# Late modulation blocks of a conditioned transformer block gathered in one step of the first body, and part of the first q stack issued from ScalarE

## The chip, the cores and the metric

One core of a Trainium2 chip. The metric is device microseconds of one execution, from the first to the last instruction with what lies around them; the median of several executions is compared.

## The reference, cut to what matters

x is 16 batches of 224 tokens by 512; the context 16 x 750 x 512; all is fp32. Per batch:

```python
c_proj = silu(c) @ W_mod + b_mod          # (16, 512) @ (512, 3072): 6 blocks of 512
shift_a, scale_a, gate_a, shift_m, scale_m, gate_m = split(c_proj, 6)
x_norm = ln(x) * (1 + scale_a) + shift_a
q, k, v = split(x_norm @ W_qkv + b_qkv, 3)             # 16 heads of 32
x = x + gate_a * (softmax(q k^T * scale) v @ W_proj + b_proj)
x = x + cross_attention(ln(x), ln(context))
h = gelu((ln(x) * (1 + scale_m) + shift_m) @ W_mlp1 + b_mlp1)
return x + gate_m * (h @ W_mlp2 + b_mlp2)
```

shift_a and scale_a are needed before anything else. gate_a is needed at the first residual of the self-attention; gate_m, shift_m and scale_m only much later. These four are the *late* blocks here.

## The kernel before, in words

The program has a self-attention phase (the first 700 us or so), a cross-attention phase and an MLP phase, with hand-written seams. Only the self-attention phase is touched. There each of five engines (SP for DMA issues, PE, DVE, ACT, POOL) has its own program, in order, and they meet at semaphores; nothing is planned by a tool. The order is written out as a *start* (16 steps h that make k, q and v of batch 0) and then *bodies*, one per batch, of 16 steps h each, one step per head. In step h of body b PE does, in this order: the transposed scores of an earlier head (`score_t`, six heads behind), a product for another batch from the table FILL (k, q and v of batch b+1, the projection of b-1, the cross q of b-2), the scores of head h+1 (`score`), every fourth step the attention output and row sums of four heads (`pv`, `sums`), at h = 12 and 13 the transposes of x of batch b+2 (`turn_x`), every fourth step the turn of the row maxima. Bodies 0 and 1 have no products of the cross q, body 0 has no projection, so their last steps (10 to 15, and 13 to 15) are thin.

Scores need k and q *stacked*: three pieces of 32 rows per head group, copied by DMA out of `natq` and `nat` into `qst` and `kst` (`stack`, L431). The first heads of batch 0 wait for one semaphore each (`first_q[j]`).

What x of the next batches goes through: `turn_x` on PE, `modulate` on DVE, `high_x` on ACT (L1141), `low_x` on POOL (L1287). At the end of a body POOL also has `sum_p` (L1295) for each head, and from body 1 on the residual of the batch before, four operations (L1303, L1305). The product k of the next batch, the first of the next body, waits for `low_x`.

The modulation: `modulation_rows(i)` (L732) multiplies silu of the conditioning, 128 x 16 four times, by a 512 x 512 block of W_mod, and gives 16 rows of 512 in a PSUM bank. Blocks 0 and 1 are made in the start. Block 2 (gate_a) is made at the end of the start, just before the first score; block 3 (gate_m) in the last step of body 0; blocks 4 and 5 (shift_m, scale_m) in steps 13 and 14 of body 1. `gate_rows` (L1009) adds the bias on DVE; `mlp_row` copies; `turn_rows` (L739) turns the last two on PE, and their bias rows at the start; `keep_bias`, `keep_modulation` store them. SP loads block 2 early, block 3 in body 0 after the first maxima, blocks 4 and 5 at the end of body 0, and stores the two gates as soon as each is there (`store_gates`). The k product of batch 2, third step of body 1, waits for the second gate rows (`rows_done` 2).

## Time and profile before

| what | value |
|---|---|
| median of 3 runs | 2616.03 us (2615.39 to 2621.15) |
| the profiled execution | 2619.34 us, span 2617.5 us |
| PE busy / DVE / ACT / POOL | 2578.0 / 1694.1 / 1126.6 / 1275.6 us |
| mean granted clock of TensorE | 0.991 |
| start of body 0, 1, 2 (first score of the batch on PE) | 43.63, 74.93, 125.71 us |

How to read it: times are microseconds from the start of the span. PE is TensorE's matmul side, PEld its weight loads. A bracket at the end of a timeline row is the time that the engine stood idle before it and what released it. An f32 matmul shows as two records; records on PE overlap in the pipeline, so a block's length is read from its start to the start of the next. The granted clock is a share of 2.4 GHz: 1.00 or 0.50.

### The profile page before, as it was taken

What the parts mean: (1) busy time and instruction counts of PE and PEld (TensorE: products, weight loads), DVE (VectorE), ACT (ScalarE), POOL (GpSimd) and SP (SyncE); (2) the same over time, 40 slices, a digit from 0 to 9 for tenths busy, and PEclk for the clock granted to TensorE, in tenths of its full rate; (3) what the DMA queues carried; (4) which work ended last, traced back from release to release, by engine and by line L of the source; (5) the groups of instructions that cost most, each with busy time, mean ns of one, the idle gap of its engine ahead of it and who ended that gap; (6) DMA issues with size and microseconds to landing.
All of it is one profiled execution on the core that took longest, in us unless ns stands there. A gap on an engine that the chain in (4) does not pass through costs nothing.

```text
span 2617.5 us, 50236 instructions
## 1 busy us (share of the span) xinstructions
PE 2578.0 (98%) x18696; PEld 2133.6 (82%) x18696; DVE 1694.1 (65%) x3399; ACT 1126.6 (43%) x2192; POOL 1275.6 (49%) x1426
## 2 busy tenths in 40 slices
PE   8999999999999999999999999999899999999999
PEld 6688888888788888888888888887678888888887
DVE  6677777777757777777777777776764444444442
ACT  4354454444535555555555555554552221212111
POOL 1445455454436777777777777775421121220230
PEclk9999999999899999999999999999899999999999
DMA  8454545555454444444444444434521111111110
GB/s 225 128 136 125 135 120 130 129 129 132 137 148 111 115 115 112 113 114 112 117 114 116 119 113 115 121 90 102 153 94 45 37 44 34 45 49 37 45 53 17
DMA packets 193045, 269.89 MB, mean 103 GB/s; under 512 B 34788, under 2 KB 112612, under 8 KB 192788
## 3 DMA queue, kind: packets, MB, share of 16 engines
q1 hardware_dynamic: 187116, 254.16, 36.9%
q0 software_dynamic: 3264, 7.92, 0.9%
q10 hardware_dynamic: 2424, 4.61, 0.7%
q8 instruction: 150, 2.46, 0.4%
q14 instruction: 91, 0.75, 0.1%
HBM read 111.11 MB, written 36.77 MB: 56 GB/s over the span
## 4 chain that ended last, share of the span: by engine, by line
PE 69%; DVE 1%; issue 0%; DMA 0%; ACT 0%; SPq 0%; DVEq 0%; ACTq 0%
PE late_tr_ps L1793 7%; PE late_sc_ps L1779 7%; PE late_or_ps L1806 5%; PE late_even_ps L72 5%; PE late_sc_ps L72 5%; PE late_even_ps L73 5%; PE late_even_ps L74 5%; PE late_sc_ps L74 5%; PE late_sc_ps L73 5%; PE late_odd_ps L72 3%; PE late_odd_ps L74 3%; PE late_odd_ps L73 3%; PE late_tr_ps L74 2%; PE late_tr_ps L72 2%; PE late_tr_ps L73 2%; PE late_odd_ps L1740 1%
## 5 line engine op out<-in xcount | busy, mean ns | idle before, releaser
L2138 ACT ACTIVATE cross_prT<-late_tr_ps 125x448 f32<-125x448 f32 x759 | 403.0, 544 | 273.5 <-PE late_tr_ps L1793 264.6
L1965 DVE TENSOR_REDUCE cross_parts<-late_sc_ps 112x1 f32<-112x500 f32 x512 | 335.5, 663 | 221.8 <-PE late_sc_ps L1779 220.7
L2211 POOL TENSOR_TENSOR cross_part<-cross_prT 125x448 f32<-125x448 f32 x232 | 271.2, 1169 | 214.6 <-ACT cross_prT L2138 176.9
L1295 POOL TENSOR_TENSOR self_psum<-self_prT 112x224 f32<-112x224 f32 x256 | 179.0, 699 | 328.3 <-ACT self_prT L1160 319.5
L1793 PE MATMUL late_tr_ps<-cross_qst,cross_kst 98*125 98x224 f32 x1536 | 309.5, 284 | 5.4 <-ACT cross_prT L2138 4.4
L1793 PEld LDWEIGHTS late_tr_ps<-cross_qst,cross_kst 98*125 98x125 f32 x1536 | 255.3, 188 | 55.8 <-ACT cross_prT L2138 16.5
L2613 ACT ACTIVATE mlp_hv<-late_sc_ps,mlp_b 128x512 f32<-128x512 f32 x112 | 77.0, 687 | 511.5 <-PE late_sc_ps L74 497.1
L2213 POOL TENSOR_TENSOR cross_part<-cross_part,cross_prT 125x448 f32<-125x448 f32 x232 | 268.5, 1157 | 18.2
L1779 PE MATMUL late_sc_ps<-cross_kst,cross_qst 96*112 96x500 f32 (+1 forms) x1024 | 262.2, 337 | 5.2 <-PEq L99 3.3
L2527 DVE CAST mlp_hT_h<-mlp_hv 128x512 fp32r<-128x512 f32 x112 | 55.9, 499 | 301.8 <-ACT mlp_hv L2613 301.8
L1160 ACT ACTIVATE self_prT<-self_st_ps 112x448 f32<-112x448 f32 x256 | 138.4, 541 | 167.6 <-PE self_st_ps L628 166.4
L1779 PEld LDWEIGHTS late_sc_ps<-cross_kst,cross_qst 96*112 96x112 f32 x1024 | 165.2, 179 | 20.1 <-issue 3.5
L908 DVE TENSOR_REDUCE self_nmax<-self_sc_ps 112x2 f32<-112x448 f32 x256 | 154.5, 614 | 33.3 <-PE self_sc_ps L599 33.2
L72 PE MATMUL late_sc_ps<-mlp_xT_l,mlp_w_h 128*128 128x512 f32 x448 | 175.8, 393 | 0.0
L74 PE MATMUL late_sc_ps<-mlp_xT_h,mlp_w_h 128*128 128x512 f32 x448 | 175.2, 391 | 0.0
L73 PE MATMUL late_sc_ps<-mlp_xT_h,mlp_w_l 128*128 128x512 f32 x448 | 175.0, 391 | 0.0
L1967 DVE TENSOR_REDUCE cross_parts<-late_sc_ps 112x2 f32<-112x500 f32 x256 | 170.2, 665 | 0.0
L2215 POOL TENSOR_TENSOR cross_psum<-cross_part 125x224 f32<-125x224 f32 x232 | 155.6, 671 | 18.2
L1806 PE MATMUL late_or_ps<-cross_prT,cross_vt 125*32 125x224 f32 x2784 | 143.7, 354 | 0.0
L72 PE MATMUL self_pj_ps<-self_xT_l,self_wqkv_h 128*128 128x224 f32 x512 | 140.6, 275 | 2.4 <-DVE self_wm_gates L1009 1.4
L74 PE MATMUL self_pj_ps<-self_xT_h,self_wqkv_h 128*128 128x224 f32 x512 | 140.6, 275 | 0.0
L73 PE MATMUL self_pj_ps<-self_xT_h,self_wqkv_l 128*128 128x224 f32 x512 | 140.3, 274 | 0.0
(343 smaller groups left out, 6870.9 us busy)
## 6 DMA issues: line engine op xcount, KB each, us to landing
cross_kst<-cross_nat_h SPq DMA_DIRECT2D x508, 93.8 KB, 2.2
cross_kst<-cross_nat_l SPq DMA_DIRECT2D x254, 93.8 KB, 2.2
cross_qst<-qc SPq DMA_DIRECT2D x192, 112.0 KB, 2.5
cross_c_in<-in_context SPq DMA_DIRECT2D x78, 224.0 KB
self_kst<-self_nat_h SPq DMA_DIRECT2D x128, 112.0 KB, 2.3
self_qst<-self_natq_h SPq DMA_DIRECT2D x128, 112.0 KB, 3.0
self_x_in<-in_x SPq DMA_DIRECT2D x16, 448.0 KB, 3.8
self_kst<-self_nat_l SPq DMA_DIRECT2D x64, 112.0 KB, 2.2
```

What stands on the lines that cost most here:

```text
L72: pe.matmul(out, lhs[0], rhs[1], start=first, stop=False)
L73: pe.matmul(out, lhs[1], rhs[0], start=False, stop=False)
L74: return pe.matmul(out, lhs[0], rhs[0], start=False, stop=last)
L1295: pool.tensor_tensor(psum[:, j], prT[:, j, 0], prT[:, j, 1], ALU.add).then_inc(p_summed, 1)
L1779: last = pe.matmul(sc_ps[u][0:QN, at:at + cn], qst[g][0:TERMS * HD, j, t * QN:(t + 1) * QN], kst[g][j][0:TERMS * HD, c0:c0 + cn], start=Tr ...
L1793: last = pe.matmul(bank(h, c)[0:SN, m * N:(m + 1) * N], kst[g][j][:, kt * SN:(kt + 1) * SN], qst[g][:, j, :], start=True, stop=True)
L1806: last = pe.matmul(or_ps[HD * j:HD * j + HD, 0:N], vt[b.par][:, kt, h * HD:h * HD + HD], prT[:, slot(h), kt], start=kt == 0, stop=kt == ST ...
L1965: dve.tensor_reduce(parts[:, g % 2, j, u, 0:1], sc_ps[u][0:QN, 0:SHALF[0]], AX_X, ALU.max, negate=True).then_inc(maxed, 1)
L1967: dve.tensor_reduce(parts[:, g % 2, j, :, 1], sc_ps[u][0:QN, 0:QT * SHALF[1]].rearrange("p (t k) -> p t k", t=QT), AX_X, ALU.max, negate=T ...
L2138: act.activation(probabilities(b, h)[:, 2 * c:2 * c + 2], bank(h, c)[0:SN, 0:2 * N].rearrange("p (k t) -> p k t", k=2), ACT.Exp).then_inc( ...
L2211: pool.tensor_tensor(part[:], prT[:, j, 0:2], prT[:, j, 2:4], ALU.add).then_inc(pre_summed, 1)
L2213: pool.tensor_tensor(part[:], part[:], prT[:, j, 4:6], ALU.add).then_inc(pre_summed, 1)
```

## The change

Blocks 2 to 5 are now made together, at the beginning of step 10 of body 0, in one PSUM bank: silu is padded with zeros from 16 to 32 columns, and block j goes to partitions 32j to 32j+31. One DVE addition over 128 x 512 adds all biases (DMA'd into a zeroed tile before), PE turns the whole in four 128 x 128 transposes in step 15 of body 0, and DVE keeps shift and scale there. The separate blocks at the end of the start, in body 0 step 15 and in body 1 steps 13 and 14, the bias turn in the start and the stores in between are gone. Blocks 3, 4 and 5 are loaded through ACT's DMA queue in steps 2, 5 and 10 of the start. Of the first batch's q stack SP issues heads 0 and 1 of each group; heads 2 and 3 are issued by ACT in steps 8 and 9 of the start. ACT's `high_o` in body 1 waits for the gates to be stored and the rows to be turned.

```diff
-        MOD_BANK = (sc_ps[0], sc_ps[1], or_ps, pj_ps[1], pj_ps[0], pj_ps[1])
+        MOD_BANK = (sc_ps[0], sc_ps[1])
+        LATE = range(2, 6)
@@ sync
             def store_gates():
+                sp.wait_ge(rows_done, 1)
                 for n in range(2):
-                    sp.wait_ge(rows_done, n + 1)
-                    sp.dma_start(gates[n], wm_gates[0:B, n, 0]).then_inc(gates_out, 16)
+                    sp.dma_start(gates[n], late_rows[HD * n:HD * n + B]).then_inc(gates_out, 16)
+
+            def load_late_bias():
+                sp.wait_ge(padded, 2)
+                for j, i in enumerate(LATE):
+                    m = MOD[i]
+                    sp.dma_start(late_bias[HD * j:HD * j + B], b_mod[m * H:(m + 1) * H].rearrange("(a n) -> a n", a=1).broadcast_to([B, H])).then_inc(late_bias_in, 16)
...
-                if b.c == 0:
-                    load_mod(3)
...
                 if b.c == 0:
-                    load_mod(4)
-                    load_mod(5)
                     store_gates()
...
-            stack(Batch(0), q_l, natq, qst, q_stacked, (0, 0, 1))
+            stack(Batch(0), q_l, natq, qst, q_stacked, (0, 0, 1), range(2))
@@ tensor
...
-                    pe.wait_ge(bm_kept, 1)
...
+                if kind == "k" and c == 0 and part == 0 and o.c == 2:
+                    pe.wait_ge(rows_done, 1)
                 if kind == "k" and c == 1 and part == 0 and o.c == 2:
-                    pe.wait_ge(rows_done, 2)
-                if kind == "k" and c == 1 and part == 0 and o.c == 3:
                     pe.wait_ge(mod_done, 2)
...
+            def late_modulation_rows():
+
+                pe.wait_ge(v_done, v_count(Batch(1), 0))
+                for k in range(KC):
+                    for j, i in enumerate(LATE):
+                        if k == 0:
+                            pe.wait_ge(wm_in[j], 16)
+                        last = pe.matmul(pj_ps[0][HD * j:HD * j + HD, :], silu[:, k], mod_raw[i][:, k], start=k == 0, stop=k == KC - 1)
+                last.then_inc(mod_ps, 1)
...
+            def turn_late_rows():
+                pe.wait_ge(rows_done, 1)
+                pe.wait_ge(v_done, v_count(Batch(1), 1))
+                for k in range(KC):
+                    last = pe.transpose(pj_ps[1][:, k * P:(k + 1) * P], late_rows[:, k * P:(k + 1) * P], ident[:])
+                last.then_inc(mod_turned, 1)
...
                 for h in range(NH):
+                    if b.c == 0 and h == 10:
+                        late_modulation_rows()
                     for o, l in late(b, h, att, prv):
                         score_t(o, l)
+                    if b.c == 0 and h == NH - 1:
+                        turn_late_rows()
...
-                    if b.c == 1 and h in (13, 14):
-                        pe.wait_ge(proj_done, h - 12)
-                        modulation_rows(h - 9)
...
-                    if b.c == 0 and h == NH - 1:
-                        pe.wait_ge(v_done, Batch(1).n(2, 2))
-                        modulation_rows(3)
-                    if b.c == 1 and h == 15:
-                        pe.wait_ge(mlp_rows, 2)
-                        turn_rows(pj_ps[1], lambda n, k: wm_mlp[0:B, n, 0, k * P:(k + 1) * P], mod_turned)
...
-            modulation_rows(2)
             score(Batch(0), 0)
@@ vector
...
+                    if b.c == 0 and h == 10:
+                        keep_late_rows()
+                    if b.c == 0 and h == NH - 1:
                         keep_modulation()
...
+            def keep_late_rows():
+                dve.wait_ge(mod_ps, 3)
+                dve.wait_ge(late_bias_in, 16 * len(LATE))
+                dve.tensor_tensor(late_rows[:], pj_ps[0][:], late_bias[:], ALU.add).then_inc(rows_done, 1)
@@ scalar
+            def stack_first_q(j):
+                act.wait_ge(q_l, Batch(0).n(2, 2))
+                for r, s in enumerate((0, 0, 1)):
+                    act.dma_start(qst[HD * r:HD * r + HD, 0, :, j].bitcast(F32), natq[s][HD * j:HD * j + HD].bitcast(F32)).then_inc(first_q[j], 16)
...
             def high_o(b, g):
                 if g == 0:
                     wait(act, proj_ps, b.n(2, 0))
+                if g == 1 and b.c == 0:
+                    act.wait_ge(gates_out, 32)
+                    act.wait_ge(mod_turned, 2)
...
                     evict(*f)
+                if h in (2, 5, 10):
+                    load_mod({2: 3, 5: 4, 10: 5}[h])
+                if h in (8, 9):
+                    stack_first_q(h - 6)
@@ gpsimd
+            pool.memset(silu[:], 0.0).then_inc(padded, 1)
+            pool.memset(late_bias[:], 0.0).then_inc(padded, 1)
```

## Rows read from the trace of the kernel before

**Rows 1.** The page, section 1: TensorE busy, share of the span.
```profile
PE 2578.0 (98%) x18696; PEld 2133.6 (82%) x18696; DVE 1694.1 (65%) x3399; ACT 1126.6 (43%) x2192; POOL 1275.6 (49%) x1426
```

**Rows 2.** Timeline of PE: start, duration (us), line, operation, out<-in, records.
```profile
40.09 3.61 PE L732 MATMUL self_or_ps<-self_wm_gates,self_silu 128*16 128x512 f32 x8
...
75.55 6.21 PE L732 MATMUL self_pj_ps<-self_wm_gates,self_silu 128*16 128x512 f32 x8
...
116.20 3.61 PE L732 MATMUL self_pj_ps<-self_wm_mlp,self_silu 128*16 128x512 f32 x8
...
126.08 0.66 PE L739 MATMUL self_pj_ps<-shared_ident,self_wm_mlp 16*128 16x16 f32 x8
```

**Rows 3.** The same timeline: attention output and its sums, four heads at once.
```profile
65.15 0.96 PE L645 MATMUL self_or_ps<-self_prT,self_vt 112*32 112x224 f32 x16
65.93 0.56 PE L652 MATMUL self_or_ps<-self_psum,self_ones 112*32 112x224 f32 x8
```

**Rows 4.** Timeline of SP, its DMA issues before the first body.
```profile
37.85 0.59 SPq L431 DMA_DIRECT2D self_kst<-self_nat_h  x1
...
39.84 0.61 SPq L431 DMA_DIRECT2D self_qst<-self_natq_l  x1
...
41.84 0.61 SPq L431 DMA_DIRECT2D self_qst<-self_natq_l  x1
```

**Rows 5.** Timeline of PE: the scores of heads 0, 1 and 3 of batch 0.
```profile
43.63 0.47 PE L599 MATMUL self_sc_ps<-self_kst,self_qst 96*112 96x224 f32 x2
...
45.27 0.37 PE L599 MATMUL self_sc_ps<-self_kst,self_qst 96*112 96x224 f32 x2
...
48.82 0.46 PE L599 MATMUL self_sc_ps<-self_kst,self_qst 96*112 96x224 f32 x2 [0.29 <-DMA self_qst<-self_natq_l]
```

**Rows 6.** Timelines of ACT, then POOL: what x of batch 1 goes through.
```profile
40.20 0.58 ACT L1153 COPY self_vt<-self_pj_ps 112x512 f32<-112x512 f32 x1 [2.59 <-PE self_pj_ps L74]
40.68 1.03 ACT L1141 CAST self_xT_h<-self_xv 128x448 fp32r<-128x448 f32 x2
...
41.39 2.34 POOL L1287 TENSOR_TENSOR self_xT_l<-self_xv,self_xT_h 128x448 fp32r<-128x448 f32 x2 [11.49 <-ACT self_xT_h L1141]
```

**Rows 7.** DMA issues from 36 to 40 us, then from 52 to 56 us; last column us to landing.
```profile
self_kst<-self_nat_h SPq DMA_DIRECT2D x3, 112.0 KB, 2.2
self_qst<-self_natq_l SPq DMA_DIRECT2D x1, 112.0 KB, 2.7
...
self_kst<-self_nat_h SPq DMA_DIRECT2D x3, 112.0 KB, 5.4
```

**Rows 8.** Timeline of PE at the end of body 0.
```profile
69.53 0.60 PE L562 MATMUL self_tx_ps<-shared_ident,self_x_in 112*128 112x112 f32 x4 [0.88 <-DVE self_xv L839]
...
71.58 1.72 PE L645 MATMUL self_or_ps<-self_prT,self_vt 112*32 112x224 f32 x16 [0.41 <-DVE self_ou L925]
...
83.33 0.37 PE L599 MATMUL self_sc_ps<-self_kst,self_qst 96*112 96x224 f32 x2
```

**Rows 9.** Timeline of POOL, end of body 0.
```profile
73.20 2.69 POOL L1287 TENSOR_TENSOR self_xT_l<-self_xv,self_xT_h 128x448 fp32r<-128x448 f32 x2
```

**Rows 10.** Busy time by stretch: PE, PEld, DVE, ACT, POOL, granted clock (share), DMA.
```profile
70.00:72.00 2.00, 1.43 (x14) 0.91 (x16) 1.90 (x4) 0.61 (x3) 0.00 (x0) 0.65 0.57 128
...
80.00:82.00 2.00, 2.00 (x6) 0.46 (x5) 0.00 (x0) 0.00 (x0) 0.00 (x0) 0.79 1.05 408
```

**Rows 11.** Timeline of PE in body 1, step 2.
```profile
87.05 0.35 PE L72 MATMUL self_pj_ps<-self_xT_l,self_wqkv_h 128*128 128x224 f32 x1 [1.39 <-DVE self_wm_gates L1009]
```

**Rows 12.** Timeline of POOL, end of body 1: first and last of eight operations, none waiting between.
```profile
115.27 1.28 POOL L1303 TENSOR_TENSOR self_y<-self_y,self_gate 112x512 f32<-112x512 f32 x1
...
122.81 2.38 POOL L1287 TENSOR_TENSOR self_xT_l<-self_xv,self_xT_h 128x448 fp32r<-128x448 f32 x2
```

**Rows 13.** Timeline of PE around it: turn of x, and the score behind the first k product.
```profile
115.31 0.55 PE L562 MATMUL self_tx_ps<-shared_ident,self_x_in 112*128 112x112 f32 x4
...
128.31 0.37 PE L599 MATMUL self_sc_ps<-self_kst,self_qst 96*112 96x224 f32 x2
```

More of the change, by code:

```diff
@@ L180, in self_phase @@
         x_in = sb("x_in", [QN, QT, H])
-        cond, cond_e, cond_d, cond_i, silu = (sb(name, [P, KC, B]) for name in ("cond", "cond_e", "cond_d", "cond_i", "silu"))
+        cond, cond_e, cond_d, cond_i = (sb(name, [P, KC, B]) for name in ("cond", "cond_e", "cond_d", "cond_i"))
         ROWS = TERMS * HD + 2
@@ L197, in self_phase @@
         wm_gates = nc.alloc_sbuf_tensor_at("self_wm_gates", [P, 2, KC, H], F32, offset=late_at)
-        bm_gates = [nc.alloc_sbuf_tensor_at(f"self_bm_gates{n}", [B, H], F32, offset=oT_at + 4 * N * (1, KC + 1)[n]) for n in range(2)]
+        late_bias, late_rows = (nc.alloc_sbuf_tensor_at(f"self_late_{name}", [P, H], F32, offset=oT_at + 4 * N * at)
+                                for name, at in (("bias", 1), ("rows", KC + 1)))
         wm_mlp = nc.alloc_sbuf_tensor_at("self_wm_mlp", [P, 2, KC, H], F32, offset=wqc_at)
-        bm_t = sb("bm_t", [P, 2 * KC, B])
+        silu = sb("silu", [P, KC, HD])
         nat = [sb(f"nat_{s}", [P, KC, N], F32R) for s in "hl"]
@@ L273, in self_phase @@
         mod_ps, mod_rows, mod_turned, mod_done, rows_done, gates_out = (sem(s) for s in ("mod_ps", "mod_rows", "mod_turned", "mod_done", "rows_done", "gates_out"))
-        bm_gates_in, bm_turned, bm_kept, mlp_rows, even_ones, odd_ones = (sem(s) for s in ("bm_gates_in", "bm_turned", "bm_kept", "mlp_rows", "even_ones", "odd_ones"))
+        late_bias_in, padded, even_ones, odd_ones = (sem(s) for s in ("late_bias_in", "padded", "even_ones", "odd_ones"))
         filled, shaped = sem("filled"), sem("shaped")
@@ L545, in _ @@
             load_x(Batch(1))
-            for n, m in enumerate((GATE_A, GATE_M)):
-                sp.dma_start(bm_gates[n][:], b_mod[m * H:(m + 1) * H].rearrange("(a n) -> a n", a=1).broadcast_to([B, H])).then_inc(bm_gates_in, 16)
+            load_late_bias()
             load_w("p", w_proj, 0)
@@ L727, in modulation_rows, with turn_first_rows @@
                 for k in range(KC):
-                    if i < 2 and k % 2 == 0:
+                    if k % 2 == 0:
                         pe.wait_ge(first_in[i][k // 2], 16)
-                    elif k == 0:
-                        pe.wait_ge(wm_in[i - 2], 16)
-                    last = pe.matmul(MOD_BANK[i][0:B, :], silu[:, k], mod_raw[i][:, k], start=k == 0, stop=k == KC - 1)
+                    last = pe.matmul(MOD_BANK[i][0:B, :], silu[:, k, 0:B], mod_raw[i][:, k], start=k == 0, stop=k == KC - 1)
                 last.then_inc(mod_ps, 1)
-            def turn_rows(bank, src, done):
+            def late_modulation_rows():
[6 more added lines that the diff above has]
+                last.then_inc(mod_ps, 1)
+            def turn_first_rows():
                 for n in range(2):
@@ L738, in turn_rows @@
                         at = (n * KC + k) * B
[L739 to L740 removed]
+                        last = pe.transpose(st_ps[0][:, at:at + B], vt[0:B, 0, n, k * P:(k + 1) * P], ident[0:B, 0:B])
+                last.then_inc(mod_turned, 1)
[4 more added lines that the diff above has]
+                    last = pe.transpose(pj_ps[1][:, k * P:(k + 1) * P], late_rows[:, k * P:(k + 1) * P], ident[:])
+                last.then_inc(mod_turned, 1)
             def body(b, att, nxt, prv, old):
                 for h in range(NH):
+                    if b.c == 0 and h == 10:
+                        late_modulation_rows()
                     for o, l in late(b, h, att, prv):
                         score_t(o, l)
+                    if b.c == 0 and h == NH - 1:
+                        turn_late_rows()
                     work = fills(b, h, "kqvpc")
@@ L974, in body @@
                         low_w(3 * KC + h - 2)
-                    if b.c == 1 and h == 0:
-                        gate_rows(3)
-                    if b.c == 1 and h in (13, 14):
-                        mlp_row(h - 9)
-                    if b.c == 1 and h == 15:
+                    if b.c == 0 and h == 10:
+                        keep_late_rows()
+                    if b.c == 0 and h == NH - 1:
                         keep_modulation()
@@ L1018, in keep_first_modulation @@
                 dve.wait_ge(mod_done, 1)
-            def columns(bank):
-                return bank[:, 0:2 * KC * B].rearrange("p (m b) -> p m b", b=B)
-            def keep_bias():
-                dve.wait_ge(bm_turned, 1)
-                dve.tensor_copy(bm_t[:, 0:KC], columns(st_ps[1])[:, 0:KC])
-                dve.tensor_scalar(bm_t[:, KC:2 * KC], columns(st_ps[1])[:, KC:2 * KC], 1.0, None, ALU.add).then_inc(bm_kept, 1)
             def keep_modulation():
                 dve.wait_ge(mod_turned, 2)
-                dve.wait_ge(bm_kept, 1)
-                dve.tensor_tensor(mod_t[:, 2 * KC:4 * KC], columns(pj_ps[1]), bm_t[:], ALU.add).then_inc(mod_done, 1)
+                shift, scale = (pj_ps[1][:].rearrange("p (k r) -> p k r", k=KC)[:, :, HD * j:HD * j + B] for j in (2, 3))
+                dve.tensor_copy(mod_t[:, 2 * KC:3 * KC], shift)
+                dve.tensor_scalar(mod_t[:, 3 * KC:4 * KC], scale, 1.0, None, ALU.add).then_inc(mod_done, 1)
             a = Batch(0)
```

25 lines of the change are left out of this document (7 added, 18 removed).

## The prediction

> **What bounds the kernel.** I read the page first: TensorE is busy 98% of the span [rows 1], so only what PE does or waits for counts, and in the first 130 us each removed instruction has to be asked whether PE gets through earlier or merely meets its next wait. Then the timeline of PE over the blocks that go [rows 2], the rows that price their replacement [rows 3], and around each place the queue that feeds PE there: SP's issues [rows 4, 7], ACT and POOL in the start [rows 6], POOL at the end of bodies 0 and 1 [rows 9, 12]. Last the windows, for the clock [rows 10].
>
> The sum is made against the profiled execution, 2619.34 us, which is 3.3 us above the median of 2616.03. A difference of 0.2%, 5.2 us, is about what a measurement of this kernel can tell from none.
>
> **The modulation work on PE.** A block of four f32 matmuls takes 3.54 us at full clock: from 40.09 to the score at 43.63 [rows 2, 5]. Four go. That of body 0 took 6.14 us, 75.55 to 81.69, because PE had the half clock of 1.2 GHz there [rows 2, 10]. The turn in body 1, about 0.6 us, goes as well [rows 2]. Added is one block of 16 matmuls, four at a time on four strips of columns. No row shows it at 512 columns; its bounds are 3.5 us, if four strips run together, and 4 x 3.54 = 14.2 us, if they don't. The nearest row is the attention output: eight f32 matmuls of 224 columns, in the same order over four strips, start at 65.15 and the sums follow at 65.93 [rows 3]. That is 0.78 us; one by one they would take 8 x (3.54 / 4) x 224/512 = 3.1 us. So four run as one, and I take 3.6 us. The four transposes I put at 0.5 us (four transposes of a smaller tile show 0.55 us [rows 13]).
>
> The Trainium skill (TensorE: Matmul & The Clock Gate, "Measured speedup vs the span model") gives three column strips a speedup of 2.38, not 3; carried to four, my estimate from it is 3.2, the block 4.5 us and the sum 0.9 us more. The trace speaks against it: 3.1 / 0.78 is a factor of 4.
>
> If each removed piece were worth its length, PE would gain 3.54 + 6.14 + 2 x 3.54 + 0.6 = 17.4 us, plus the wait below, minus 4.1. It isn't; three places show why.
>
> **Place 1, the first score.** Without block 2 PE would reach score 0 at 40.1 instead of 43.63. But the last k piece is issued at 37.85 and lands 2.2 us later, at 40.1; the last piece of q head 0 is issued at 39.84 and lands 2.7 us later, at 42.5 [rows 4, 7]. So at best 1.1 us is left. Next comes k of batch 1, which needs `low_x` of batch 1. Before, ACT evicts v at 40.20, does both `high_x` from 40.68, and POOL ends at 41.39 + 2.34 = 43.7, just as PE arrives [rows 6]. Now ACT's queue holds, between that evict and `high_x`, three stack issues and one load. An issue of a stack costs SP 0.6 us [rows 4]; on ACT no row of this stage shows it, so bounds are nothing and 0.6; I take 0.6, the same DMA. Then `high_x` starts at about 42.6, its second half's `low_x` ends at 45.5, and the k product, whose last half (0.67 us) waits for it, ends at 46.2 instead of at 45.27 [rows 5]: 0.9 us **later**. The wait of 0.29 us at head 3 goes [rows 5]. Net +0.6 us. Bounds: -1.4 us (ACT's issues cost nothing, so only q head 0 counts), and +4 us: block 4's load of 1 MB is now under way while the first stacks move. Where block 3's load went just ahead of k stacks, from 52.88, they landed 5.4 us after issue instead of 2.2 [rows 7]; 3.2 us more on q head 0 puts score 0 at 45.7, and q head 1, issued at 41.84, at 47.7.
>
> The Trainium skill (DMA: Bandwidth & Descriptors, "Issuing engines are not separate DMA queues") says that DMAs from SP and ACT run on the same 16 DMA engines and interleave, so that a second issuer saves issue time alone. By it the q rows of heads 2 and 3 delay those of heads 0 and 1, and the sum goes towards +2. The landings of [rows 7] show transfers of one queue that delay each other; no row shows two queues.
>
> **Place 2, end of body 0.** The late block comes in at 64.55 or so and moves all behind it by 3.6 us. Behind it PE waits for chains that don't shorten: 0.88 us for DVE, 0.41 us for the attention output [rows 8]. In the last step block 3 has covered POOL: `low_x` of batch 2 ends at 73.20 + 2.69 = 75.9 [rows 9], and PE came to k of batch 2 only behind it. Without the block, k's second half waits for 75.9 + 3.6 = 79.5 and the step ends at 80.2, not at 83.33 [rows 8]: -3.1 us, and of the 6.14 us removed that is all after the late block is paid. This holds at full clock. Had PE had it before too, the step would have ended at 83.33 - 4.6 = 78.7 (block 3 2.6 us shorter, and some 2.0 us of what stands between 71.58 and 75.55), so against an execution without the slow stretch this place **costs** 1.5 us.
>
> **The wait in body 1.** PE stood 1.39 us for the gate rows, which came behind a reciprocal on DVE [rows 11]. Those rows are now made in body 0: -1.4 us. New is ACT's wait for the stored gates before `high_o` of group 1. SP stores them after the last maxima, about 80; even a landing of 4 us ends near 84, ACT is due there at about 82.7 (behind the second k product), and its next exponentials are asked for two steps of 1.6 us on: nothing on PE. DVE's addition over 128 x 512 (0.68 us as the 16-row one) lies beside attention output and sums. Padding, bias rows and the removed bias turn lie under the first loads and DVE's weight splits: nothing.
>
> **Place 3, end of body 1.** Blocks 4 and 5 and the turn fill 7.7 us there. Yet POOL runs from 115.27 to 122.81 + 2.38 = 125.2 without a gap: two residuals, two sums, both `low_x` [rows 12]; it starts with PE's transposes at 115.31 and doesn't hang on the blocks. PE would be ready for k of batch 3 at about 121.8: 126.08 [rows 2] less the two blocks, 119.0, and some 2.8 us of waits for DVE that the blocks hid (in body 0 0.88, 0.41 and more [rows 8]). It waits, k's second half starts at 125.2, the step ends at 125.9 instead of 128.31 [rows 13]: -2.4 us of 7.7.
>
> **Sum at full clock:** 2619.34 + 0.6 - 3.1 - 1.4 - 2.4 = 2613.0 us (rounded).
>
> **The clock.** Before, the granted clock fell to half once here, near 70.6, after waits of 0.88 us and less in the thin end of body 0, and stayed so to near 80.8: the windows give 0.65 for 70 to 72 and 0.79 for 80 to 82 [rows 10]. With less work and longer waits both thin ends get sparser: in body 1 PE would idle some 5 us of 9. I take it that the clock falls there. Inside the thin end POOL's wait hides that; the k products behind it run at half speed until it is given back. From both ends: nothing, and half of 10.2 us (a stretch as long as the one before, all of it on products), 5.1. I take the middle, 2.6. In body 0 the same may return and outlast 80.2; there at most half the stretch does, so the bounds are 0 and 2.6, and I take 0.8, since POOL's wait hides its beginning. Forecast: 2613.0 + 3.4 = **2616.4 us**.
>
> **Rivals.** (1) *Removed work counts in full*: PE-bound throughout, POOL and stacks catch up. It gives 2619.34 - 17.4 - 1.4 + 4.1 = 2604.6. For it speaks PE's 98%; against it [rows 9, 12], which no shorter PE moves. 0.2, with half-way outcomes below 2610.8. (2) *Slower: the strips don't run together* at 512 columns. Place: step 10 of body 0; price up to 14.2 - 3.6 = 10.6, so 2626.6; it decides from a block of 8.8 us on. [rows 3] speaks against it. 0.05. (3) *The change doesn't give the q rows earlier*: the load through ACT delays the first stacks, place 1 at +4, and 2619.8; with both slow stretches at their long ends 2624. 0.25 in all, 0.1 of it beyond 2621.3. The forecast has 0.5.
>
> **Numbers.** Low end: full clock throughout and place 1 at -1.4 give 2611.0, and a part of rival 1 reaches to 2608. High end: place 1 at +4 and half the long stretches, 2622. Faster by over 0.2% (below 2610.8) 0.21, within 0.64, slower 0.15.
>
> **What would show it.** Right: the late block takes 3.5 to 3.7 us; score 0 starts after 42.5, and PE or `low_x` of batch 1 is later than before; k of batches 2 and 3 stands behind POOL's `low_x` by about 1.5 us and 2 to 3; the 1.39 us wait is gone; granted clock 0.5 near the end of body 1. Wrong: PE goes into k of batch 3 without an idle bracket, or the first score of body 2 comes more than 10 us earlier than before, or the late block takes over 5 us.

## The result: 7.5 us slower, all of it lost before score 4 of batch 0

| | before | after |
|---|---|---|
| median of 14 runs each, us | 2615.52 (2612.52 to 2621.15) | 2623.02 (2621.85 to 2624.91) |
| ratio after / before | | 1.0028, 95% interval 1.0021 to 1.0035 |
| profiled execution, us | 2619.34 | 2624.22 |
| its span, us, and granted clock | 2617.5, 0.991 | 2622.3, 0.989 |

Predicted were 2616.4 us and a range of 2608 to 2622, with 0.64 for "no difference". The kernel is slower by 0.28%, which is the outcome "slower by over 0.2%" that had 0.15, and outside the range. The interval is 0.07% to either side, so this comparison tells smaller differences than the 0.2% that the prediction took for its limit.

The page's section 1 of after, for [rows 1]:

```profile
PE 2570.8 (98%) x18684; PEld 2137.7 (82%) x18684; DVE 1691.4 (65%) x3395; ACT 1126.6 (43%) x2192; POOL 1277.4 (49%) x1428
```

PE is busy for 7.2 us less and the span is 4.8 us longer: 12 us of idle time are new in this execution. The timeline of PE in after tells where (columns as in [rows 5], which holds these scores of before):

```profile
48.51 0.68 PE L603 MATMUL self_sc_ps<-self_kst,self_qst 96*112 96x224 f32 x2 [7.86 <-DMA self_qst<-self_natq_l]
...
52.39 0.72 PE L603 MATMUL self_sc_ps<-self_kst,self_qst 96*112 96x224 f32 x2 [0.64 <-DMA self_qst<-self_natq_l]
...
58.00 0.37 PE L603 MATMUL self_sc_ps<-self_kst,self_qst 96*112 96x224 f32 x2
...
73.67 0.62 PE L742 MATMUL self_pj_ps<-self_wm_gates,self_silu 128*32 128x512 f32 x2
...
77.24 0.46 PE L631 MATMUL self_st_ps<-self_qst,self_kst 98*112 98x224 f32 x2
...
84.28 1.23 PE L647 MATMUL self_or_ps<-self_prT,self_vt 112*32 112x224 f32 x16 [0.75 <-DVE self_ou L934]
...
86.70 1.05 PE L756 MATMUL self_pj_ps<-shared_ident,self_late_rows 128*128 128x128 f32 x4
...
89.83 0.37 PE L603 MATMUL self_sc_ps<-self_kst,self_qst 96*112 96x224 f32 x2
...
120.20 0.55 PE L566 MATMUL self_tx_ps<-shared_ident,self_x_in 112*128 112x112 f32 x4
...
128.35 0.34 PE L72 MATMUL self_pj_ps<-self_xT_l,self_wqkv_h 128*128 128x224 f32 x1 [1.44 <-POOL self_xT_l L1296]
...
130.90 0.57 PE L603 MATMUL self_sc_ps<-self_kst,self_qst 96*112 96x224 f32 x2
...
136.82 0.37 PE L603 MATMUL self_sc_ps<-self_kst,self_qst 96*112 96x224 f32 x2
```

Score 0 comes 4.9 us later than in [rows 5], behind a wait of 7.86 us for q rows; score 1 comes 7.1 us later, score 3 9.2 us. Score 4 starts at 59.57 against 50.49, 9.1 us later. From there the lag shrinks: 6.5 us at 89.83 (83.33 in [rows 8]), 4.9 at 120.20 and 2.6 at 130.90 ([rows 13] for both). Then it grows once more, to 5.0 at 136.82 (131.83 before), about the difference of the spans.

Of the 9.1 us, 0.5 were there before any of this: the transposes of x in step 8 of the start began at 38.72 in after and at 38.21 in before. Over all profiled executions that point lies between 38.21 and 40.03, also for kernels with the same instructions up to there (38.21 in before, 39.02 in g2), so times of score 4 are compared below from that point on. By that the start costs 8.6 us.

Busy time by stretch in after (columns as in [rows 10]):

```profile
44.00:48.00 4.00, 0.00 (x0) 0.00 (x0) 0.00 (x0) 0.53 (x2) 2.25 (x2) 0.50 1.12 230
48.00:52.00 4.00, 3.24 (x14) 3.00 (x14) 0.62 (x1) 0.00 (x0) 0.00 (x0) 0.50 1.07 310
...
128.00:132.00 4.00, 3.42 (x18) 3.27 (x19) 1.48 (x6) 0.12 (x1) 3.56 (x6) 0.65 0.63 193
132.00:136.00 4.00, 4.00 (x21) 4.00 (x21) 2.73 (x6) 1.92 (x5) 0.66 (x1) 0.50 0.63 186
```

PE does nothing at all from 44 to 48 while the DMA engines are full (the last column but one). The half level of 1.2 GHz stands from about 44, some 3 us into the wait, to about 57.4; before had 2.4 GHz there throughout.

Why the rows are late shows in the DMA views of after. First the queues in 32 to 36 us (packets, MB, share of 16 engines), where q1 is SP's and q10 is ACT's, with one line of the issues of this stretch:

```profile
q10 hardware_dynamic: 670, 1.34, 99.0%
q1 hardware_dynamic: 6, 0.02, 1.3%
...
self_kst<-self_nat_h SPq DMA_DIRECT2D x5, 112.0 KB, 5.6
```

Then issues of 40 to 44 us (median us to landing in the last column):

```profile
self_wm_mlp<-in_w_mod ACTq DMA_DIRECT2D x1, 1024.0 KB, 11.3
...
self_qst<-self_natq_l SPq DMA_DIRECT2D x2, 112.0 KB, 7.5
```

SP issued a k stack every 0.6 us in the first of these, and in 4 us only six packets of its queue moved. The loads of 1 MB on ACT's queue had the engines almost to themselves. The k stacks land 5.6 us after issue and the last pieces of the q stacks 7.5, against 2.2 and 2.7 in [rows 7].

ACT's and POOL's timelines in after, for [rows 6]:

```profile
40.70 1.31 ACTq L1111 DMA_DIRECT2D self_qst<-self_natq_h  x2
42.05 0.68 ACTq L1111 DMA_DIRECT2D self_qst<-self_natq_l  x1
42.77 0.64 ACTq L1115 DMA_DIRECT2D self_wm_mlp<-in_w_mod  x1
43.50 1.03 ACT L1143 CAST self_xT_h<-self_xv 128x448 fp32r<-128x448 f32 x2 [2.23 <-issue]
...
44.21 2.33 POOL L1296 TENSOR_TENSOR self_xT_l<-self_xv,self_xT_h 128x448 fp32r<-128x448 f32 x2 [13.77 <-ACT self_xT_h L1143]
```

### The profile page after: what moved, and what is told of

Same layout as the page of the kernel before. It is cut to its first block, busy times and chain, and to the rows that moved or that the text cites. A ratio compares the mean times of both kernels' runs of the same rounds, so it can differ in the third digit from the quotient of the medians.

```text
span 2622.3 us, 50208 instructions
## 1 busy us (share of the span) xinstructions
PE 2570.8 (98%) x18684; PEld 2137.7 (82%) x18684; DVE 1691.4 (65%) x3395; ACT 1126.6 (43%) x2192; POOL 1277.4 (49%) x1428
## 4 chain that ended last, share of the span: by engine, by line
PE 68%; SPq 1%; DVE 1%; issue 0%; DMA 0%; ACT 0%; DVEq 0%
PE late_tr_ps L1804 7%; PE late_sc_ps L1790 6%; PE late_or_ps L1817 5%; PE late_sc_ps L72 5%; PE late_even_ps L72 5%; PE late_sc_ps L74 5%; PE late_sc_ps L73 5%; PE late_even_ps L74 5%; PE late_even_ps L73 5%; PE late_odd_ps L72 3%; PE late_odd_ps L74 3%; PE late_odd_ps L73 3%; PE late_tr_ps L74 2%; PE late_tr_ps L72 2%; PE late_tr_ps L73 2%; PE late_odd_ps L1751 1%
```

## The experiments

Each of the fourteen kernels has the median of 11 executions (f1 of 6, f2 of 9); before is given with the median of the same session. "Score 4" is the start of the fifth score of batch 0 in the one profiled execution, "from the transposes" the same counted from the transposes of x in step 8 of the start.

### The queues, one at a time

**e1: loads of blocks 3 to 5 back on SP.** After, with

```
# ACT, start
-                if h in (2, 5, 10):
-                    load_mod({2: 3, 5: 4, 10: 5}[h])
# SP, body 0, behind place_maxima(b, 0)
+                    for i in (3, 4, 5):
+                        load_mod(i)
```

> The changed kernel with one thing different: the loads of blocks 3, 4 and 5 go back to SP's queue, behind the first row maxima of body 0, where block 3's load stood before. Theory L (the 1 MB loads in ACT's queue in the start run ahead of SP's stacks, which then land 5 to 8 us after issue): the stacks land 2.2 to 3 us after issue again, score 0 starts between 42.5 and 43.7 us instead of 48.5, PE has no half clock near 50, and the time is 2613 to 2616, that is 7 to 10 us under the changed kernel and 0 to 2 us under the kernel before. Theory Q (it is the q rows of heads 2 and 3 in ACT's queue that delay those of heads 0 and 1): score 0 stays behind 46 us and the time at 2619 or more.

**e2: q rows back on SP,** the loads stay on ACT's queue:

```
-                if h in (8, 9):
-                    stack_first_q(h - 6)
-            stack(Batch(0), q_l, natq, qst, q_stacked, (0, 0, 1), range(2))
+            stack(Batch(0), q_l, natq, qst, q_stacked, (0, 0, 1))
```

> The changed kernel with the first batch's q stack all on SP again, the loads of blocks 3 to 5 still in ACT's queue. Theory L: q head 0 still lands 6 us or more after issue, score 0 starts at 46 to 49, the half clock follows, the time stays at 2621 to 2625. Theory Q: score 0 comes to about 43 us, the time to 2614 to 2617.

**e3 and e4: each transfer put alone into the kernel before.** e3 adds `stack_first_q` for heads 2 and 3 on ACT and cuts SP's stack to two heads; e4 adds ACT's three loads in steps 2, 5 and 10 of the start and drops SP's.

> The kernel before with only the q rows of heads 2 and 3 issued by ACT; modulation and loads as before. Theory L: score 0 starts within 0.5 us of 43.6, the wait of 0.29 us at head 3 goes, low_x of batch 1 ends some 2 us later than 43.7 and costs PE about 1 us; time within 1.5 us of the kernel before. Theory Q: score 0 at 45 or later, time 2 us or more above the kernel before.

> The kernel before with only the loads of blocks 3, 4 and 5 moved to ACT's queue in steps 2, 5 and 10 of the start; all modulation work where it was, the q stack on SP. Theory L: the stacks land 5 us or more after issue, score 0 starts at 46 to 49 us although block 2 stands before it, PE waits 3 to 5 us for it; time 4 to 9 us above the kernel before. Theory Q: nothing changes, within 1 us of the kernel before.

**f5: both transfers back on SP,** block 2 still out of the start (e1's and e2's edits together).

> The kernel after, with both transfers put back on SP's queue: all q rows of batch 0 as in the kernel before, and the loads of blocks 3 to 5 behind the first maxima of body 0. Block 2 stays out of the start. If the 9.1 us lost by score 4 come from what ACT's queue carries (both the loads and the q rows): q head 0 lands near 42.5, score 0 starts there behind a wait of about 2 us, score 4 starts at 49.5 to 50.5 instead of 59.57 (e1, with the q rows alone still on ACT's queue, had 54.62), and the median is near 2615.3, about 4.4 below e1's. Rival (the removed block itself is the loss: the wait that it covered brings half the granted clock whatever the queues do): half clock in the windows from 42 to 52, score 4 at 52.5 or later, median at 2618 or above.

| | loads | q rows of heads 2, 3 | block 2 in the start | median, us | before in that session | ratio, interval | score 4, us | from the transposes, us |
|---|---|---|---|---|---|---|---|---|
| after | ACT | ACT | no | 2623.02 | 2615.52 | 1.0028, 1.0021 to 1.0035 | 59.57 | 20.85 |
| e2 | ACT | SP | no | 2619.72 | 2615.71 | 1.0014, 1.0006 to 1.0023 | 56.13 | 17.76 |
| e1 | SP | ACT | no | 2619.72 | 2615.71 | 1.0013, 1.0004 to 1.0022 | 54.62 | 15.36 |
| f5 | SP | SP | no | 2616.45 | 2616.56 | 1.0003, 0.9994 to 1.0012 | 52.13 | 12.64 |
| e4 | ACT | SP | yes | 2621.99 | 2615.71 | 1.0023, 1.0014 to 1.0032 | 57.71 | 18.70 |
| e3 | SP | ACT | yes | 2620.73 | 2615.71 | 1.0017, 1.0008 to 1.0026 | 52.48 | 13.68 |
| before | SP | SP | yes | | | 1 | 50.49 | 12.28 |

With both transfers on SP no loss is left that the medians can show, and 0.4 of the 8.6 us in the trace. Putting one of the two back on SP gives 3.3 us of median (e1, e2 against after). The one that then remains is 3.3 us of median above f5 as well, but by the ratios that is 0.10 to 0.11%, with intervals that overlap. The traces part them: from the transposes to score 4 the loads cost 5.1 us (e2 against f5), the q rows 2.7 (e1 against f5), and the two sum to 7.8 of the 8.2 between f5 and after. My expectation for one cause was wrong: I had set the loads against the q rows, and both hold. For f5, 1.3 us of its score 4 at 52.13 instead of 49.5 to 50.5 is the later start; the half clock that its rival named is there, the rival's 2618 or more is not.

e3 and e4 have each transfer with the rest of the change absent, and both are slower than before: by 5.0 and 6.3 us of median, by 1.4 and 6.4 in the trace up to score 4. For e3 the two don't agree. Its profiled execution was its fastest (2616.87 us; the other ten go from 2618.35 to 2622.81), so where the rest of its 5.0 us goes is not shown. That the two medians sum to 11.3 and not to 7.5 stays open with it.

The waits at the first scores, from the timelines of PE of e1, e2, e4 (score 1) and f5:

```profile
45.42 0.69 PE L606 MATMUL self_sc_ps<-self_kst,self_qst 96*112 96x224 f32 x2 [4.21 <-DMA self_qst<-self_natq_l]
```
```profile
46.76 0.69 PE L603 MATMUL self_sc_ps<-self_kst,self_qst 96*112 96x224 f32 x2 [6.45 <-DMA self_qst<-self_natq_l]
```
```profile
50.44 0.71 PE L595 MATMUL self_sc_ps<-self_kst,self_qst 96*112 96x224 f32 x2 [3.04 <-DMA self_qst<-self_natq_l]
```
```profile
43.56 0.43 PE L606 MATMUL self_sc_ps<-self_kst,self_qst 96*112 96x224 f32 x2 [2.12 <-DMA self_qst<-self_natq_l]
```

How the q rows alone do it shows in the queues and issues of 40 to 44 us of e3, and below them the one queue of before in the same stretch:

```profile
q10 hardware_dynamic: 530, 0.43, 48.9%
q1 hardware_dynamic: 495, 0.46, 47.9%
...
self_qst<-self_natq_h SPq DMA_DIRECT2D x4, 112.0 KB, 4.1
self_qst<-self_natq_h ACTq DMA_DIRECT2D x2, 112.0 KB, 4.0
```
```profile
q1 hardware_dynamic: 874, 0.70, 80.4%
```

Here two queues with the same stacks share the engines evenly: the rows of heads 2 and 3, which are needed last, move beside those of heads 0 and 1, and all land after about 4 us where one queue took 2.3. More moves in the 4 us (0.90 MB against 0.71), but not what is needed first: the second queue takes the order away.

There is a second part. SP's first two issues of q stacks, in e3 and then in e4:

```profile
39.29 2.00 SPq L431 DMA_DIRECT2D self_qst<-self_natq_h  x2
```
```profile
39.29 1.32 SPq L431 DMA_DIRECT2D self_qst<-self_natq_h  x2
```

Where ACT issues its q stacks in the same stretch they take SP 1.78 to 2.12 us (after, e1, e3, f1, f2); in the other kernels, e2 and e4 with full DMA engines among them, 1.32. So the third piece of q head 0 is also issued some 0.7 us later.

### What the exposed wait costs by itself

**f4: f5 with work in block 2's place,** 16 f32 matmuls of 128 columns that nobody reads, before score 0:

```
+            filler(pe, or_ps, ident, 16)
             score(Batch(0), 0)
```

> f5 with 16 plain f32 matmuls of 128 columns (32 passes, about 3.6 us by the 0.114 us a pass of f1) before the first score, in the place of block 2. If the removed block is worth what it hid: score 0 at 43.7, score 4 at 50.5 as in the kernel before, median within 1 us of f5's. Rival (the exposed wait starts the half clock): f5 is slower than this one by 2 us or more.

Measured: 2616.56 us (ratio 0.9999, 0.9990 to 1.0008), f5's 2616.45. Score 0 started at 44.49, score 4 at 51.67, and from the transposes score 4 took 12.45 us for f5's 12.64. f5's profile does have a stretch at half clock behind its wait of 2.12 us (0.68 in 44 to 48, 0.90 in 48 to 52). Counted from the transposes its score 0 is 1.2 us earlier than f4's (4.07 against 5.27), and from score 0 to score 4 it is 1.4 us slower (8.57 against 7.18): the half clock takes back what the earlier score gave. Block 2 was worth nothing in the start, neither as work to remove nor as cover, as long as the stacks came on time.

**f1: after, with 36 such matmuls in the wait of 7.86 us.**

> The kernel after, with 36 plain f32 matmuls of 128 columns on TensorE between the last product of the start and the first score: they write a bank that nobody reads and lie inside the wait of 7.86 us. Theory C (the exposed wait makes the granted clock fall, and that carries about half of the 9.1 us lost by score 4): score 0 still starts near 48.5, the windows from 44 to 60 us show a granted clock near 1.0, score 4 starts near 56 instead of 59.57, and the median is near 2619.5 (3.5 below after's 2623.0). Rival D (scores 1 to 4 wait for their stacks, so the clock hides behind DMA): score 4 stays within 1 us of 59.5, more idle brackets for DMA appear before scores 1 to 3, and the median stays at 2622 to 2623.

```profile
54.05 0.46 PE L609 MATMUL self_sc_ps<-self_kst,self_qst 96*112 96x224 f32 x2 [2.48 <-DMA self_qst<-self_natq_l]
```
```profile
52.00:56.00 4.00, 1.95 (x13) 1.95 (x14) 0.62 (x1) 0.00 (x0) 0.00 (x0) 0.88 0.46 115
56.00:60.00 4.00, 4.00 (x28) 4.00 (x27) 2.09 (x5) 1.31 (x3) 0.00 (x0) 0.70 0.00 0
```

Measured: 2624.73 us over six executions (ratio 1.0031, 1.0019 to 1.0044), no gain. The clock stayed full over the whole wait (windows 40 to 52 at 1.00), and then PE stood 2.48 us for head 1's rows: at half clock the product between scores 0 and 1 had only filled that wait. Score 4 started at 60.43, but this start was 1.3 us later as a whole (the transposes ahead at 40.03 instead of 38.72), so 0.4 us were gained. So theory C falls: the clock is not half of the 9.1 us. Up to score 1 the landing of head 1's rows sets the time (7.1 us), whatever the clock is. Only the 2.0 us from there to score 4 (7.18 us in after from score 1 to 4, 5.22 before) are the clock's, and f1, with 6.38, lost 1.2 of them again in a new half-clock stretch behind its new wait.

### The parts that the prediction had priced

**g2: the gate row's addition moved out of body 1,** in the kernel before:

```
-                    if b.c == 1 and h == 0:
+                    if b.c == 0 and h == NH - 1:
                         gate_rows(3)
```

> The kernel before, with the second gate row's addition on DVE done at the end of body 0 instead of in step 0 of body 1. If the 1.39 us wait of body 1 is lost time by itself (my term for it): the wait is gone, and the median is 1.4 below before's, near 2614.3. Rival: the wait turns up at the next place, and the median stays within 0.4 of before's 2615.7.

Measured: 2614.16 us, 1.3 below before's 2615.50 in that session; ratio 0.9997, 0.9989 to 1.0006. Its timeline shows no idle bracket between 80 and 112 us, where [rows 11] has 1.39. The size is as expected, but the interval takes in no change, so it isn't shown by the times.

**g4: g2, with blocks 4 and 5 together on two strips** in step 13 of body 1, start and loads as before:

```
+                for k in range(KC):
+                    for i in (4, 5):
...
+                        at = HD * (i - 4)
+                        last = pe.matmul(pj_ps[0][at:at + B, :], silu[:, k], mod_raw[i][:, k], start=k == 0, stop=k == KC - 1)
```

> The kernel before, with the gate row as in g2, and blocks 4 and 5 taken together on two strips of columns in step 13 of body 1 (one block of 3.54 us instead of two); start, loads and q rows as in before. If place 3 is as I priced it (POOL's low_x sets the end of body 1, at most 2.4 us to be had) and the clock holds: TensorE stands some 0.5 to 1.2 us for low_x before the second half of k of batch 3, score 4 of body 2 starts 3.8 us before the kernel before's 135.06, at 131.3, and the median is near 2611.9. Rival 1: the whole 3.54 us counts, 2610.8 and no wait for POOL. Rival 2: the thinner end costs the clock its full level, a stretch at half clock from 126 us on, and 2.4 us are given back: 2614.3.

```profile
111.50 0.55 PE L562 MATMUL self_tx_ps<-shared_ident,self_x_in 112*128 112x112 f32 x4
...
112.40 3.61 PE L742 MATMUL self_pj_ps<-self_wm_mlp,self_silu 128*16 128x512 f32 x16
```

Measured: 2615.18 us, ratio 0.9999 (0.9990 to 1.0007). Two blocks took 3.61 us, as one of [rows 2] did. In the profiled execution the end of body 1 is shorter by what I priced, from the transposes at 111.50 to the score at 122.23, 10.7 us against 13.0 in [rows 13]. It has no bracket for `low_x`, though; PE waits 0.90 us for DVE instead. In the median nothing is left of it. Score 4 of body 2 started 4.4 us earlier than in g2, half of it because g4 had the full clock at the end of body 0 and g2 had not. After 600 us its trace has thirteen windows of 4 us with a granted clock under 0.97 and g2's nine, and the span is 0.5 us longer than g2's. Whether that is chance or follows from the edit isn't settled by one profile each.

**f2: after, with matmuls in the idle time of the end of body 1** (5 in each of steps 13 and 14, 7 in step 0 of body 2):

> The kernel after, with 5 plain f32 matmuls of 128 columns in each of steps 13 and 14 of body 1 and 7 in step 0 of body 2, into banks that are free there: TensorE is busy in waits that it would have anyway. Theory C2 (the half clock from 129 to 136 us costs 2.4 us, and it comes from the idle time in the thin end of body 1): granted clock near 1.0 in 128 to 140, score 4 of body 2 at 137.6 instead of 140.06, median near 2620.6. Rival: the clock falls all the same, or the added matmuls put TensorE behind POOL's low_x: score 4 of body 2 at 140 or later, median 2623 or above.

```profile
84.00:88.00 4.00, 2.73 (x35) 1.99 (x36) 2.63 (x8) 1.84 (x4) 2.98 (x3) 1.00 0.63 138
...
128.00:132.00 4.00, 4.00 (x39) 4.00 (x38) 3.00 (x7) 0.55 (x2) 3.52 (x6) 1.00 0.52 153
132.00:136.00 4.00, 4.00 (x50) 3.29 (x49) 3.07 (x8) 3.53 (x7) 0.92 (x2) 1.00 0.74 223
```

The profiled execution has the full clock at both thin ends and score 4 of body 2 at 136.74 instead of 140.06, and took 2616.97 us. But the median of nine is 2622.45 (ratio 1.0025, 1.0016 to 1.0035), 0.6 below after's: the profiled one was the fastest. That the half clock costs some 2.4 us there where it occurs is shown; that these matmuls keep it away is not. The window 84 to 88 has no added work and was at full level here too.

### Four versions meant to beat both

**h1: one late block at the end of body 0,** where block 3 stood, its turn at the end of body 1, q rows on SP, the loads issued by ACT in body 0 (and `high_o` waits for the late rows alone):

```
+                    if b.c == 0 and h in (0, 3, 4):
+                        load_mod({0: 3, 3: 4, 4: 5}[h])
```

h2 is h1 with 9 of f4's matmuls before score 0.

> A version meant to beat both: the kernel after with all q rows on SP's queue, the loads of blocks 3 to 5 issued by ACT in steps 0, 3 and 4 of body 0 (behind the first stacks, between the maxima rows), the late block at the end of body 0 where block 3 stood (into the other bank; its rows in the memory of block 4's weights), its turn at the end of body 1. If places 1 to 3 are as the runs so far show them: score 4 at 49.5, the late block at the end of body 0 costs what block 3 cost, the 1.39 us wait is gone, the end of body 1 gives 2.4 us by POOL's low_x, and if the half clock at that end takes 2.4 back the median is 2613.1, if not 2610.7. Rival: the loads on ACT's queue delay the maxima rows or the k stacks of batch 1, with waits for DMA before the first late scores; then 2615 or above.

> h1 with 9 plain f32 matmuls of 128 columns (about 2.05 us) before the first score, inside its wait of about 2 us. If the clock holds over that wait by itself: the same median as h1 within 0.6 us. If h1 shows half clock after it: 2 us below h1.

Measured: 2622.03 and 2620.05 us (ratios 1.0017, 1.0009 to 1.0026, and 1.0015, 1.0007 to 1.0024). The rival held. PE's and ACT's timelines of h1:

```profile
41.01 0.43 ACTq L1115 DMA_DIRECT2D self_wm_gates<-in_w_mod  x1
...
48.74 0.72 PE L603 MATMUL self_sc_ps<-self_kst,self_qst 96*112 96x224 f32 x2 [2.27 <-DMA self_qst<-self_natq_l]
...
62.98 0.51 PE L631 MATMUL self_st_ps<-self_qst,self_kst 98*112 98x224 f32 x2 [2.59 <-DMA self_qst<-self_mrow_l]
```

I had meant the first load to come behind the first stacks; ACT issued it at 41.01, ahead of q rows. The other two, at 55.7, came just before the maxima rows at 56.4. h1 and h2 differ by 2 us in the medians, but their intervals overlap.

**h3: the loads on SP, later:** block 3's behind the first maxima as in before, blocks 4's and 5's behind the third; **h4** adds 9 matmuls in the start and 5 in each of steps 13 and 14 of body 1.

> h1 with block 3's load where the kernel before had it (SP, behind the first maxima of body 0) and the loads of blocks 4 and 5 on SP behind the third maxima, so that no load of 1 MB stands ahead of a stack or a maxima row that TensorE is about to need. If the late block itself is worth what places 2 and 3 and the wait give, and f5's 1.78 us and f4's 2.32 us for the maxima rows were the loads' doing: no DMA wait over 0.5 us between score 1 and the end of body 0, score 4 of body 0 at 51 to 52, the 1.39 us wait gone, the end of body 1 earlier by 2.4 us, median 2613 to 2615 (before 1.5 to 3.5 above). Rival: the late block waits for the loads at the end of body 0, or the half clock at the two thin ends takes the gain back; then 2616 or above and DMA named before the late block, or clocks of 0.5 near 80 and near 125.

> h3 with 9 plain f32 matmuls of 128 columns before the first score (inside its wait of about 2 us) and 5 in each of steps 13 and 14 of body 1. If the clock is what is left: full clock from 40 to 60 and from 115 to 130 us, median 1 to 2.5 below h3's. Rival: TensorE's fillers change nothing or come on top, median at h3's or above.

Measured: 2620.25 and 2620.96 us (1.0012, 1.0003 to 1.0021, and 1.0014, 1.0005 to 1.0023). h3's time lies where its rival had it, but the largest wait is one that neither side had named; for h4 the rival held. In h3 score 4 came at 53.21, for the 51 to 52 expected, and PE stood 7.15 us in front of a score of batch 1:

```profile
83.39 0.68 PE L608 MATMUL self_sc_ps<-self_kst,self_qst 96*112 96x224 f32 x2 [7.15 <-issue]
```

The DMA view of 60 to 92 us of h3 (a digit of the first line is the busy share of 0.8 us) tells why:

```profile
DMA  9999999266661660669999999999000000000011
...
self_wm_mlp<-in_w_mod SPq DMA_DIRECT2D x2, 1024.0 KB, 6.5
self_qst<-self_natq_h SPq DMA_DIRECT2D x8, 112.0 KB, 5.2
```

The two loads, issued at 72.03, stand ahead of the last q stacks of batch 1, issued at 73.06 to 76.41; the engines are full from 74.4 to 82.4, and the score starts 1 us behind that. The profile names no releaser for the bracket; by the program this score waits for the k and q stacks of batch 1. h4 has the same wait, 6.89 us, behind loads issued at 70.19, so though its clock was full from 44 to 60 and from 116 to 132, where h3's fell to half in both, no gain shows. f4 and f5 have the same thing with the loads at 54 to 56, ahead of k stacks and maxima rows: 2.32 and 1.78 us of waiting for maxima rows. From the timeline of f5:

```profile
71.63 0.46 PE L634 MATMUL self_st_ps<-self_qst,self_kst 98*112 98x224 f32 x2 [1.78 <-DMA self_qst<-self_mrow_l]
```

So of the kernels run none beats before by more than the measurement can tell; g2 is the nearest to it.

## Why the prediction was wrong, by its steps

- **Place 1, net +0.6 us, failed.** It was 9.1 us at score 4, 8.6 of them the start's own. The step that failed is its bound: "3.2 us more on q head 0 puts score 0 at 45.7, and q head 1 [...] at 47.7". I had counted one load under way while the first stacks move, and taken its price from a load in the same queue ([rows 7]), which delays what is behind it once. Three errors stand in that. Three loads were moved, issued at 25.97, 31.23 and 42.77, and around the second, just ahead of the first k stack at 31.38, the k stacks landed 2.6 to 3.4 us late. A load in the other queue is not ahead once: in 32 to 36 us that queue took nearly the whole bandwidth (99% against 1.3%), and in 40 to 44, with the third load behind q rows, about half of it (47.9% against 61.2%). And head 1's rows, not head 0's, are the last that PE waits for; they move beside those of heads 2 and 3 and the third load. The sum needed all stacks of the start, not the last piece of head 0 alone. Its upper bound of +4 doesn't follow from its figures either: score 1 at 47.7 against 45.27 is 2.4.
- **The q rows,** which I took to give nothing and to cost ACT some issue time, cost 2.7 us up to score 4 by their place in a second queue (e1 against f5; 1.4 in e3). The term for ACT was nearly right: 0.65 to 0.82 us a stack issue for my 0.6; `high_x` at 43.50 for my 42.6, `low_x` ending at 46.5 for my 45.5. It came to nothing behind the later score 0.
- **Which rule bore it out.** The Trainium skill (DMA: Bandwidth & Descriptors, "Issuing engines are not separate DMA queues"), by which I said the sum would go towards +2, had the direction, and e3 agrees with it by 4.1 us for 2.3. In 32 to 36 us of after no interleaving shows, with 99.0% against 1.3%. I gave it too little, since I asked only what the q rows do by it and not what the loads do.
- **Rival 3** ("the load through ACT delays the first stacks") named the larger part of the mechanism, with 0.25 and a place 1 of +4. The q rows' part isn't in it, and its size was off by more than half.
- **The late block:** 73.67 to 77.24, 3.57 us for the 3.6 taken. Rival 2 falls (its 2626.6 was counted from the median of before; from the forecast it is 2627.0). The 3.2-fold speedup that I had carried over to four strips from the Trainium skill (TensorE: Matmul & The Clock Gate, "Measured speedup vs the span model") and that would make 4.5 us falls with it: four strips at 512 columns ran as one, 4 x 3.54 / 3.57, a factor of 4.
- **Place 2:** -3.1 predicted, -2.6 measured (a lag of 9.1 at score 4, 6.5 at 89.83). The number is near by luck, for POOL was not what bound there: `low_x` of batch 2 ended at 88.59, k's second half started at 89.16, and no bracket stands before it. Two executions with the full clock in this stretch show what did. The first lines are g4's, whose body 0 is that of before up to the gate row's addition, the last two f2's, whose body 0 is after's:

```profile
75.60 0.43 PE L599 MATMUL self_sc_ps<-self_kst,self_qst 96*112 96x224 f32 x2 [1.15 <-issue]
...
81.14 0.37 PE L599 MATMUL self_sc_ps<-self_kst,self_qst 96*112 96x224 f32 x2
```
```profile
87.52 0.43 PE L609 MATMUL self_sc_ps<-self_kst,self_qst 96*112 96x224 f32 x2 [1.27 <-issue]
...
89.34 0.37 PE L609 MATMUL self_sc_ps<-self_kst,self_qst 96*112 96x224 f32 x2
```

In both PE stands over 1 us in front of the first score of batch 1, which by the program waits for that batch's stacks (the profile names no releaser). From score 4 to the last of these scores g4 takes 29.74 us (51.40 to 81.14) and f2 30.07 (59.27 to 89.34). So at full clock place 2 costs 0.3 us, not the 1.5 of the prediction: the late block and its turn add 4.0 up to the first score of batch 1, and behind it block 3 gives back its whole length.
- **The wait in body 1:** -1.4 predicted, -1.6 measured (6.5 at 89.83, 4.9 at 93.36, where before had its score at 88.46). g2 has it alone.
- **Place 3:** -2.4 predicted. The lag falls from 4.9 to 2.6 us, so -2.3, and POOL binds as said, with the bracket of 1.44 us. POOL's timeline of after, for [rows 12], without a gap from the first to the last of these:

```profile
120.17 1.27 POOL L1312 TENSOR_TENSOR self_y<-self_y,self_gate 112x512 f32<-112x512 f32 x1
...
127.07 2.35 POOL L1296 TENSOR_TENSOR self_xT_l<-self_xv,self_xT_h 128x448 fp32r<-128x448 f32 x2
```

- **The clock:** 2.6 us in body 1 predicted, 2.4 measured (the lag rises from 2.6 at 130.90 to 5.0 at 136.82, in the windows of 0.65 and 0.50). In body 0 the half level stood from about 85 to 88, inside place 2's -2.6; f2, without it, was only 0.2 us quicker there.
- **What cancels.** Against its own profiled execution the change gives -2.6 - 1.6 - 2.3 + 2.4 = -4.1 us behind score 4, against +9.1 up to it: +5.0, and the spans differ by 4.8. Before's profiled execution is not a typical one: its median lies 3.8 us lower. It took 32.84 us over place 2 (50.49 to 83.33), with half clock from 70.6 to 80.6; g2, e3 and e4, with the same work for PE there, took 31.85 to 32.15 with shorter stretches, and g4 29.74 with none. The forecast carried this with it: it was summed from the profiled execution and held against the median. With full clock in place 2 the change is worth 8.6 + 0.3 - 1.6 - 2.3 + 2.4 = 7.4 us, against g2, e3 and e4 5.2 to 5.5; the medians say 7.5. Which of before's executions have the stretch, and how often after loses the clock in body 1, no run shows, so that the first of the two sums fits so well is no proof.

Of the signs named beforehand most were there: the late block's length, score 0 after 42.5, `low_x` later, no 1.39 us wait, the half clock in body 1, and for POOL at batch 3 a wait of 1.44 us, where 2 to 3 were named. They were signs of the mechanisms and not of the size of place 1, for which "score 0 starts after 42.5" left everything open. The wait for POOL at k of batch 2, named with 1.5 us, was missing.

## What to carry to other kernels

Before a load is moved forward, list every transfer that is issued or in flight until it has landed, on all queues, and for each who waits for it: in this kernel's first 80 us each new place for these weights (26 to 43 us, 41 to 56, 54 to 57, 72) had small transfers behind or beside it that TensorE then waited for, and only the two loads at 77 in before, behind all of them, show no such wait. A second queue didn't make the small transfers of this start earlier; it let others in between, and the order in one queue is worth keeping where it is the order of need. And where removed work stood in front of a wait, look for the wait first: of the 7.7 us of work at the end of body 1 2.3 were gained, of the 3.5 in the start nothing.

## What the hardware showed that I had not expected

- A load of 1 MB in ACT's queue was not interleaved evenly with stacks of 112 KB in SP's: 1.34 MB against 0.02 MB in the same 4 us. In 40 to 44 us, with q rows on both queues and a load behind them, both were late alike (6.2 and 5.3 us). And the load of 31.23 us was no longer moving much in 36 to 40 (0.08 MB on ACT's queue), while the stacks kept up in that stretch (0.97 MB) and still landed 4.8 us after issue.
- After's three loads on ACT's queue landed 8.6, 9.3 and 11.3 us after issue. The stacks beside them went from 2.2 to as much as 7.5.
- SP's own issues grew longer while ACT issued q stacks too: two of them took 2.03 us in after at 39.76 and 1.32 in before at 38.48. Full engines alone don't do it: e2 and e4 show 1.32 with the DMA engines as full as in after.
- Four blocks of f32 products of 512 columns on four strips cost what one does (3.57 against 3.54 us), two on two strips as well (3.61).
- The same kernel keeps or loses the clock from one execution to the next: f2's nine runs go from 2616.97 to 2626.72, and the profiled ones have stretches at the half level between 668 and 712 us (not e4's and f2's), between 764 and 804, and between 1820 and 1904, that differ in number and length.
